# Three fp32r passes in place of fp32 in the output projection of a cross attention

## The reference, cut to what matters

```python
attn = jax.nn.softmax(scores, axis=-1)
ctx_c = jnp.einsum('bhsl,bld->bhsd', attn, kv_r)          # 16 heads, 64 latent features
ctx_lat = jnp.einsum('bhsd,hkd->bhsk', ctx_c, w_kc_kv)
ctx = ctx_lat.transpose(0, 2, 1, 3).reshape(Bv, Sv, H * K)
return ctx @ Wo.T                                          # then x = layernorm(x + ...)
```

## Time and profile before

| | |
|---|---|
| median of three executions | 898.0 us |
| the profiled execution, its own time | 901.3 us |
| its span | 899.5 us |
| mean granted TensorE clock | 0.986 of full speed |
| TensorE matmul busy | 848.8 us, 94% |
| TensorE weight loads | 668.4 us, 74% |
| VectorE | 635.6 us, 71% |
| ScalarE | 281.1 us, 31% |
| GpSimd | 126.5 us, 14% |
| `project`, L1478, TensorE busy | 60.0 us, 256 records |
| `context` evictions, L853, ScalarE busy | 18.8 us, 32 |

### The profile page before, as it was taken

One profiled execution on the slowest core, in us unless ns is written; L12 is line 12 of the kernel. 1 busy time (PEld: TensorE's weight loads), 2 busy tenths in 40 slices (PEclk: granted clock), 3 DMA queues, 4 the chain that ended last, 5 costly groups with the idle time before them and its releaser, 6 DMA issues.

```text
span 899.5 us, 14653 instructions
## 1 busy us (share of the span) xinstructions
PE 848.8 (94%) x5696; PEld 668.4 (74%) x5696; DVE 635.6 (71%) x1390; ACT 281.1 (31%) x502; POOL 126.5 (14%) x101
## 2 busy tenths in 40 slices
PE   5999999999999999999797999999999999999994
PEld 4967677776777768776566788888888888888873
DVE  3565787878878888779687866656665666666557
ACT  4521153112432124211354423233332323232232
POOL 2014400343013330134122100000000000000021
PEclk9999999999999999999998999999999999999997
DMA  9210000100001000000310041020302020000001
GB/s 346 107 36 2 1 2 1 32 17 17 1 1 48 1 16 1 0 25 4 128 58 24 1 140 52 22 65 1 111 23 65 0 86 36 23 1 1 1 23 71
DMA packets 12686, 35.84 MB, mean 40 GB/s; under 512 B 1488, under 2 KB 2384, under 8 KB 12112
## 3 DMA queue, kind: packets, MB, share of 16 engines
q1 hardware_dynamic: 12624, 34.98, 11.1%
HBM read 30.33 MB, written 2.36 MB: 36 GB/s over the span
## 4 chain that ended last, share of the span: by engine, by line
PE 83%; DVE 11%; issue 3%; ACT 2%; DMA 0%; POOL 0%; ACTq 0%; DVEq 0%
PE ps L243 21%; PE ps L244 20%; PE ps L245 20%; PE ps L1398 6%; PE ps L1478 4%; PE ps L1469 2%; PE ps L1280 2%; PE ps L1454 1%; PE ps L1316 1%; PE ps L1234 1%; DVE small L255 1%; DVE small L1079 1%; PE ps L1445 1%; PE ps L1345 1%; DVE stats L923 1%
## 5 line engine op out<-in xcount | busy, mean ns | idle before, releaser
L500 DVE TENSOR_TENSOR su<-sg,ps 128x512 f32<-128x512 f32 x96 | 66.0, 688 | 134.4 <-PE ps L245 133.2
L243 PE MATMUL ps<-y_hi,f_hi 128*128 128x512 f32 x384 | 150.6, 392 | 0.0
L244 PE MATMUL ps<-y_lo,f_hi 128*128 128x512 f32 x384 | 150.1, 391 | 0.0
L245 PE MATMUL ps<-y_hi,f_lo 128*128 128x512 f32 x384 | 150.1, 391 | 0.0
L370 ACT ACTIVATE sg<-ps 128x512 f32<-128x512 f32 x96 | 57.4, 598 | 264.4 <-PE ps L245 264.4
L723 POOL TENSOR_TENSOR roped<-prod 128x512 f32<-128x512 f32 x64 | 81.0, 1288 | 175.3 <-DVE prod L1024 175.3
L1024 DVE TENSOR_TENSOR prod<-ps,ropeq 128x512 f32<-128x512 f32 x128 | 79.3, 681 | 27.9 <-PE ps L245 27.3
L245 PEld LDWEIGHTS ps<-y_hi,f_lo 128*128 128x128 f32 x384 | 72.5, 189 | 15.3
L243 PEld LDWEIGHTS ps<-y_hi,f_hi 128*128 128x128 f32 x384 | 72.5, 189 | 14.9
L244 PEld LDWEIGHTS ps<-y_lo,f_hi 128*128 128x128 f32 x384 | 72.4, 189 | 15.0
L243 PE MATMUL ps<-xT_hi,a_hi 128*128 128x512 f32 x192 | 78.8, 410 | 2.1 <-DVE xT_lo L949 2.1
(11 more groups left out here) (157 smaller groups left out, 1369.5 us busy)
## 6 DMA issues: line engine op xcount, KB each, us to landing
cb<-routing SPq DMA_DIRECT2D x32, 256.0 KB
f_raw<-in_L_ffn_gate_up_proj SPq DMA_DIRECT2D x8, 768.0 KB, 5.2
f_raw<-in_L_ffn_down_proj SPq DMA_DIRECT2D x8, 384.0 KB, 5.8
xb<-in_x SPq DMA_DIRECT2D x4, 512.0 KB, 4.2
lq<-in_L_xattn_Wq SPq DMA_DIRECT2D x1, 2048.0 KB, 14.4
x2T_all<-in_L_xattn_Wo SPq DMA_DIRECT2D x1, 2048.0 KB, 8.3
x2T_all<-x2T SPq DMA_DIRECT2D x4, 512.0 KB, 3.2
out<-res SPq DMA_DIRECT2D x4, 512.0 KB, 2.6
```

The lines of the kernel that those rows point to most:

```text
L243: pe.matmul(dst, l_hi, r_hi, start=first, stop=False, skip_group_check=check)
L244: pe.matmul(dst, l_hi, r_lo, start=False, stop=False, skip_group_check=check)
L245: return pe.matmul(dst, l_lo, r_hi, start=False, stop=last, skip_group_check=check)
L500: dve.tensor_tensor(su[:, k % 2], sg[:, k % 2], bank(2 * (k % 2) + 1), ALU.mult).then_inc(s_su, 1)
```

## The change

The folded weights become two fp32r tiles, `u_hi` and `u_lo`; the evicted context becomes `ct_hi` and `ct_lo`. ScalarE writes the high parts in the place of `u_w` and `ct`. VectorE gets new subtractions: four `u_lo_out` in `linear(0)`, and two halves of `context_lo` for each of four tiles in each of four cross stages. `project` becomes 24 fp32r matmuls. Waits on `s_ct` become waits on `s_ctl`, which counts low parts. `fold_u` uses four PSUM banks and no longer waits for its evictions. Tiles are shrunk or share space to make room.

```diff
-    c_all = sb(ctx, "c_all", [P, BLOCKS * TILES, EXPERTS])
+    c_all = sb(ctx, "c_all", [P, (BLOCKS - 1) * TILES, EXPERTS])
...
-    u_w = sb(att, "u_w", [P, PAIRS, D])
-    roped = sb(att, "roped", [P, 2, 4, BT])
+    u_hi = sb(att, "u_hi", [P, PAIRS, D], F32R)
+    u_lo = sb(att, "u_lo", [P, PAIRS, D], F32R)
+    rope_space = ExitStack()
+    roped = sb(rope_space, "roped", [P, 2, 4, BT])
+    rope_space.close()
+    at = sb(att, "at", [P, 2, PAIRS, P])
+    ct_hi = sb(att, "ct_hi", [P, PAIRS, P], F32R)
+    ct_lo = sb(att, "ct_lo", [P, PAIRS, P], F32R)
...
-    small = sb(att, "small", [P, 160])
+    small = sb(att, "small", [P, 96])
...
+    u_bank = lambda i: (4, 5, 0, 1)[i]
...
-                    pe.wait_ge(s_ct, 8 * BLOCKS)
+                    pe.wait_ge(s_ctl, 8 * BLOCKS)
...
+        def u_lo_out(i):
+            dve.wait_ge(s_u, i + 1)
+            r = slice(2 * i, 2 * i + 2)
+            dve.tensor_tensor(u_lo[:, r, :], bank(u_bank(i)).rearrange("p (r d) -> p r d", d=D),
+                              u_hi[:, r, :].bitcast(F32), ALU.subtract).then_inc(s_ulo, 1)
+
+        def context_lo(b, t):
+
+            for h in range(2):
+                dve.wait_ge(s_ct, 8 * b + 2 * t + h + 1)
+                o = slice(64 * h, 64 * h + 64)
+                dve.tensor_tensor(ct_lo[:, :, o], bank(4 + h).rearrange("p (r s) -> p r s", s=SEQ),
+                                  ct_hi[:, :, o].bitcast(F32), ALU.subtract).then_inc(s_ctl, 1)
...
             norm1(b)
+            for i in range(PAIRS // 2):
+                u_lo_out(i)
             xT_lo_out(b, 0, s_x1hi, s_x1lo)
...
                 shift(b, 1)
                 silu(n, 1)
                 silu(n, 2)
+                context_lo(b, 0)
                 normalise(b, 1)
                 silu(n, 3)
                 shift(b, 2)
...
                 residual2(b, 0, 4)
                 normalise(b, 2)
                 silu(n, 5)
+                context_lo(b, 1)
                 norm2(b, 0)
                 shift(b, 3)
...
                 normalise(b, 3, (1,))
+                context_lo(b, 2)
                 gated(n, 0)
...
                 residual1(n, 1)
+                context_lo(b, 3)
                 norm1(n)
...
                 shift(b, 0)
                 normalise(b, 0)
                 shift(b, 1)
+                context_lo(b, 0)
                 normalise(b, 1)
                 shift(b, 2)
                 residual2(b, 0, 6)
+                context_lo(b, 1)
                 normalise(b, 2)
                 shift(b, 3)
                 residual2(b, 1, 6)
                 normalise(b, 3)
+                context_lo(b, 2)
                 norm2(b, 0)
                 norm2(b, 1)
                 residual2(b, 2, 6)
+                context_lo(b, 3)
                 norm2(b, 2)
...
-                if i >= 2:
-                    pe.wait_ge(s_u, i - 1)
+                if i == 2:
+                    pe.wait_ge(s_alo, PAIRS * KC)
...
-            pe.wait_ge(s_u, PAIRS // 2)
+            pe.wait_ge(s_ulo, PAIRS // 2)
             pe.wait_ge(s_alo, PAIRS * KC)
             turn_kv(b, 0, KV_BANKS[0])
...
                     if not following and t >= 1:
-                        pe.wait_ge(s_ct, 8 * b + 2 * t)
+                        pe.wait_ge(s_ctl, 8 * b + 2 * t)
...
-                pe.wait_ge(s_ct, 8 * b + 2 * t + 2)
+                pe.wait_ge(s_ctl, 8 * b + 2 * t + 2)
...
                 for c in range(PAIRS):
-                    mm = pe.matmul(ps[:, f, 0:D], ct[:, c, :], u_w[:, (c + 4 * (t // 2)) % 8, :],
-                                   start=c == 0, stop=c == PAIRS - 1)
+                    i = (c + 4 * (t // 2)) % 8
+                    mm = split_matmuls(pe, ps[:, f, 0:D], ct_hi[:, c, :], ct_lo[:, c, :], u_hi[:, i, :], u_lo[:, i, :],
+                                       c == 0, c == PAIRS - 1)
                 mm.then_inc(s_uo, 1)
```

More of the change, by code:

```diff
@@ L118, in build @@
     flat = roped[:, :, :, :].rearrange("p a b n -> p (a b n)")
-    at = flat[:, 0:2048].rearrange("p (k r s) -> p k r s", k=2, s=P)
-    ct = flat[:, 2048:3072].rearrange("p (r s) -> p r s", s=P)
     raw_wq = lq[:, :, :].rearrange("p r n -> p (r n)").rearrange("p (h c) -> p h c", h=16)
@@ L180, in build @@
     s_mps, s_m = sem("m_in_psum"), sem("m_ready")
-    s_ups, s_u = sem("u_in_psum"), sem("u_ready")
+    s_ups, s_u, s_ulo = sem("u_in_psum"), sem("u_hi_ready"), sem("u_lo_ready")
     s_xb, s_xbfree = sem("x_loaded"), sem("x_buffer_free")
@@ L201, in build @@
     s_tp, s_at = sem("weightsT_in_psum"), sem("weightsT_ready")
-    s_av, s_ct = sem("latent_ctx_in_psum"), sem("latent_ctx_ready")
+    s_av, s_ct, s_ctl = sem("latent_ctx_in_psum"), sem("latent_ctx_hi_ready"), sem("latent_ctx_lo_ready")
     s_uo, s_r2, s_x2 = sem("xattn_out_in_psum"), sem("xattn_residual_ready"), sem("x2_ready")
@@ L804, in linear @@
                 act.wait_ge(s_ups, i + 1)
-                act.activation(u_w[:, 2 * i:2 * i + 2, :], bank(4 + i % 2).rearrange("p (r d) -> p r d", d=D), ACT.Copy)\
+                act.activation(u_hi[:, 2 * i:2 * i + 2, :], bank(u_bank(i)).rearrange("p (r d) -> p r d", d=D), ACT.Copy)\
                     .then_inc(s_u, 1)
@@ L852, in context @@
                     act.wait_ge(s_av, 8 * b + 2 * t + h + 1)
-                    act.activation(ct[:, :, 64 * h:64 * h + 64], bank(4 + h).rearrange("p (r s) -> p r s", s=SEQ),
+                    act.activation(ct_hi[:, :, 64 * h:64 * h + 64], bank(4 + h).rearrange("p (r s) -> p r s", s=SEQ),
                                    ACT.Copy).then_inc(s_ct, 1)
@@ L1329, in fold_u @@
                         head = 4 * (c % 4) + 2 * h + c // 4
-                        mm = pe.matmul(ps[64 * h:64 * h + 64, 4 + i % 2, (c % 2) * D:(c % 2 + 1) * D],
+                        mm = pe.matmul(ps[64 * h:64 * h + 64, u_bank(i), (c % 2) * D:(c % 2 + 1) * D],
                                        raw_kv[:, head, :], raw_wo[:, head, :], start=True, stop=True)
@@ L1408, in pairs @@
                     pe.wait_ge(s_r2, 4 * b)
-                    pe.wait_ge(s_ct, 8 * b)
+                    pe.wait_ge(s_ctl, 8 * b)
                 if p >= 2:
@@ L1483, in xout @@
                 if following:
-                    pe.wait_ge(s_ct, 8 * b + 6)
+                    pe.wait_ge(s_ctl, 8 * b + 6)
                 if t >= 1:
@@ L1529, in cross @@
                 turn_kv(n, 0, KV_BANKS[0])
-                pe.wait_ge(s_ct, 8 * b + 8)
+                pe.wait_ge(s_ctl, 8 * b + 8)
                 turn_kv(n, 1, KV_BANKS[1])
```

## The result

Five executions of the changed kernel took 922.52 to 927.09 us, median **924.4 us**; five of the kernel before, on the same chip, 897.95 to 900.02, median 899.8. The ratio is 1.0282 (1.0264 to 1.0300): slower, as forecast, and inside the range of 906 to 926, 6.4 us above the 918.0 given. The profiled execution took 922.5 us (span 920.7) against 901.3 (899.5). The span grew by 21.2 us where the sum of the prediction said 20.0; the medians differ by 24.6, because the profiled execution of before was one of its long ones and that of after one of its short ones.

The account below looks back on a forecast made before the run. TensorE was taken to lead three cross stages slightly, a VectorE, ScalarE, TensorE chain to bound the last. Block 0's 2.0, three repeated stages' 6.0 and the last's 12.0 gave +20.0 us: 921.3 profiled, 918.0 median, range 906 to 926.

Parts of the forecast that it names:

- TensorE's term: All 16 project calls: 3.45 us becomes 2.85, gaining 0.60 a call, 9.6 in all if TensorE ends every wait.
- (a): Last cross stage: normalise(1) waits behind context_lo(0) for ScalarE's eviction of context(0), +2.8 us.
- (b): Last cross stage: normalise(1)'s multiply is held by GpSimd's y_lo, +1.8 us, in all +4.6.
- (c): Last cross stage: context(1) is evicted later, then its context_lo follows, so normalise(2) comes at +7.7 us.
- (d): Last cross stage: normalise(3) at +7.1 us, context_lo(2) adds 1.24, so norm2(0) comes at +8.3.
- (e): Last cross stage: GpSimd's later f_lo now holds norm2(0) for about 5.0 us, in all +9.6.
- (f): Last cross stage: context_lo(3) brings norm2(2) to +10.8 us.
- term (g), the clock: Last cross stage: TensorE's idle waits lower its clock, slowing project(0) and project(1), counted as 1.2 us in all.
- Rival A: Whole kernel faster: VectorE's slack covers context_lo, TensorE remains the bound, -9.6 us, 888.4; chance 0.08.
- Rival C: TensorE's clock falls more often, in three repeated stages (+3 us) and the last (+4), 925 in all; chance 0.14.
- Rival B: Slower by less: GpSimd holds nothing new, last stage +6 us, the others +1, 908 in all; chance 0.14.
- The rule weighed: VectorE instructions with two SBUF inputs contend with GpSimd ones reading SBUF, others don't; context_lo is never held.

Follow-up runs that it names:

- e1: Changed kernel with all 32 context_lo left out, project's third pass taking the high part of the context twice: 900.7 us, ratio 1.0008 to the kernel before.
- e8: Changed kernel with every context_lo and its waits kept, but each subtracting 8 of 512 columns; project takes ct_hi for ct_lo: 912.9 us, ratio 1.0155.
- e9: Changed kernel without context_lo(3) in the three repeated cross stages, where project(3) takes the high part twice: 924.2 us, ratio 1.0256.
- e3: Changed kernel with context_lo left out of the last cross stage alone: 908.6 us, ratio 1.0088.
- e4: Changed kernel with 28, 16 and 24 identity transposes added ahead of turn(1), turn(2) and xout(0) in the last cross stage: 920.7 us, ratio 1.0223.
- e5: Changed kernel with GpSimd's y_lo moved later in the last cross stage and f_lo run in three parts: 912.6 us, ratio 1.0151.

## Why the prediction came out as it did

**VectorE's terms** were right: 0.69 us a half, +1.2 for a pair, +3.5 at `norm1`, 1.5 given back beside `diagonal`, **+2.0 us a repeated stage**, measured 2.0 three times over. e1, e8 and e9 bear out its parts one by one: work 2.3 and waits 0.85, less 1.1 for the faster projects; the given-back stretch returns when `norm1` is early.

**TensorE's term**: 2.95 us for `project(0)` in place of 2.85, and its gain unused as said. That it is used so little (1.1 us of 2.4 a stage with no `context_lo` at all) was not foreseen for e1.

**Block 0**: +1.75 us from the start of `norm1` to `cross(0)` (predicted +2.0). The transposes of x1 follow `norm1` at the same distance as before (4.51 us and 4.50), so it is added behind them, where the `u_lo` stand; e1, without `context_lo`, has 1.76. In e3, e4 and e9 it was 2.3 to 2.4. The table shows +0.75 because `norm1` itself began 1.0 us earlier in this profiled execution (48.82 for 49.82), and that is TensorE's clock: the steps of the first projection fell from 0.43 to 0.24 us at about 16 us, in the kernel before not until its end. The same matmul in the kernel before and in the changed one:

```profile
16.63 0.63 PE L244 MATMUL ps<-xT_lo,w_hi 128*128 128x512 f32 x1
...
16.35 0.40 PE L249 MATMUL ps<-xT_lo,w_hi 128*128 128x512 f32 x1
```

The edits don't touch this stretch, and in e3, e4 and e9 `norm1` begins at 49.7 to 49.9 again: this 1.0 us was luck of one execution.

**The last stage**, predicted +12.0, measured +13.45. By its steps, each less the 7.67 us of the stage's start: (a) `normalise(1)` +2.9, predicted 2.8; (b) +4.5, predicted 4.6; (c) `normalise(2)` +8.4, predicted 7.7; (d) `norm2(0)` +10.3, predicted 8.3; (e) the hold 5.01 us, predicted 5.0; (f) `norm2(2)` +13.7, predicted 10.8. The step that was mis-sized is **term (g), the clock**: I priced it at 1.2 us for the two projects, and by e4 it costs 3.4, 2.2 by `context(2)` and 1.2 more with `context(3)`, which I had not counted. The waits behind it were not as said either: TensorE is idle 3.51 us ahead of `turn(1)`, but 1.88 ahead of `turn(2)` where I had some 3, and the third wait that matters, 2.94 us ahead of `xout(0)`, I had not named. Without the 3.4 `norm2(2)` would stand at +10.3 where the steps had 10.8, so the rest of the sum holds to half a microsecond, a little too high. Add 3.4, and take off 0.2 (from `norm2(2)` to the first logits matmul it was 14.7 us instead of 15.0), and the stage is the measured 13.45, 1.4 over the 12.0.

**The pairs stage of block 1**, priced at nothing, cost +0.9 once: after 1.22 us of idle time ahead of the transposes of x1 the clock was at 0.52 from 166 to 168. The same idle time in blocks 2 and 3 had no such effect, nor in any of the three blocks in e3 and e4. So it belongs to this execution more than to the change, and cancels most of the 1.0 us of luck in block 0: the 21.2 us of span are near the truth by two accidents of opposite sign. Rival C had asked for this fall in all three stages; it came in one, and rival C's other half, the clock of the last stage, was mostly real. The truth lies between the forecast and C, and so does the time.

**The median**: 918.0 rested on the three runs shown, whose median lay 3.3 us below the profiled execution. The five beside the changed kernel had 899.8: 1.8 us of the 6.4 missed. The span's growth, 21.2 for 20.0, is 1.2. The rest, 3.4, is that the profiled execution of before lay 1.5 above its median and that of the changed kernel 1.9 below.

**One reading of the prediction was wrong** without touching its sum: "were nothing held, ... the stage +10.2" takes out (b) alone. It leaves the new 5.0 us of (e) in, and the 3.90 of the kernel before in the comparison. e5, with holds of at most 1.8 us, came to 57.2, +4.2 over the kernel before.

Rival A falls by e1: not even with `context_lo` at nothing does TensorE's saving show beyond 1.1 us a stage, so the point at which it decides, 0.3 us a half, was near (e8, at 0.17 us a half, is at -0.2 a stage) but its price of 9.6 us was far too high. Rival B fell by the last stage. The rule weighed, of the Trainium skill, SBUF — State Buffer, "Who interferes with whom", held for the operations that the sum used: `context_lo`, whose other input is PSUM, kept its 0.69 us where it ran wholly beside `diagonal` (159.22, above) and in e5 beside a third of `f_lo` (481.49), while the multiply with two SBUF inputs took 2.32 us and the one on a single column 5.01. For an operation with at most one SBUF input the same section of the Trainium skill excepts VectorE's 2-port modes, which the prediction left out. The last point below is a case that the short form of the rule would miss; no run here shows in which mode it ran.

## What to carry to other kernels

A saving on the engine with the highest busy share is worth only what the waits leave of it: here 9.6 us became under 4 in the stages (e1: three times 1.1, and 0.5) and nothing in e1's median, and the price, 24 us of small operations on another engine, fell into a chain that had no filler. Before splitting an operand, ask which engine makes the low part, where in its order, and for which eviction it waits; in a chain without other work the wait costs more than the operation. And look at what a shift pushes small operations into: moving GpSimd's long subtractions out of VectorE's way was worth more (6 us in the unchanged kernel) than the faster arithmetic.

## What was not expected of the hardware

- The wait ahead of which the clock falls and the work that then runs at 1.2 GHz are different instructions. 4.3 us of the last stage came back when TensorE transposed its identity through three idle stretches (e4), though those 68 transposes compute nothing; 1.6 of the 4.3 came in matmuls that were slow before the change too.
- The same stretch of idle time does not always lower it. After 1.22 us it fell in block 1 and not in blocks 2 and 3, nor in e3 and e4; the last stage of e9, in code equal to the change's, took 3.5 us longer. Executions of one kernel differ likewise: e1's ten fell into two groups, 898.6 to 898.9 and 902.5 to 903.6 us. A difference of 2 us between totals is within this, and so is one of 3.5 between last stages; the repeated stages agree to 0.15 us within each run.
- An operation with one SBUF input beside GpSimd stretched as well: `TENSOR_SCALAR` on 128x4 took 0.75 us beside `diagonal` (e9) and 0.17 in the changed kernel, where `diagonal` was over; one on 128x256 took 5.27 us beside `f_lo` (e8, at 477.17), 0.41 in other places. The 128x4 operation of two inputs took 1.13 and 0.16.
